# FFN batch norm of a decoder layer on one core: last statistics from PSUM, the average inside an expert product, and the fourth expert product behind the first scores

## The reference

```
xn   = layernorm(x)
q    = (xn @ Wq + bq) as (B, S, 8 heads, 64)
mean, var = moments of q over batch, token and head      # 64 features
q    = (q - mean) / sqrt(var + eps) * gamma + beta
s0, s1 = l2norm(q[:32]) . l2norm(key0), l2norm(q[32:]) . l2norm(key1)   # 32 + 32 scores per head
top 4 of each -> 16 pairs per head, softmax over the 16 sums -> weights w
eh   = gelu(down[idx] . xn)                 # exact gelu
out  = sum over heads and pairs of up[idx] * eh * w
x    = x + out
```

## Time and profile before

| | |
|---|---|
| median of 3 runs | 404.35 us (404.19 to 405.8) |
| span of the profiled execution | 403.8 us (a device time of its own is not given) |
| PE busy | 395.0 us (98%) |
| DVE, ACT, POOL busy | 300.1 us (74%), 237.8 us (59%), 215.9 us (53%) |
| the chain that ended last, by engine | PE 80%, POOL 12%, DVE 4%, issue 3%, DMA 1% |
| mean granted TensorE clock | 0.992 of full |

### The profile page before, as it was taken

How to read it: one execution, slowest core, us unless ns; L and a number is a source line. 1 busy time by engine, 2 the same in 40 slices (tenths; PEclk the granted TensorE clock), 3 DMA queues, 4 the chain that set the end, 5 groups by cost and what they waited for, 6 DMA issues and landing times.

```text
span 403.8 us, 7801 instructions
## 1 busy us (share of the span) xinstructions
PE 395.0 (98%) x2584; PEld 367.1 (91%) x2584; DVE 300.1 (74%) x1093; ACT 237.8 (59%) x519; POOL 215.9 (53%) x209
## 2 busy tenths in 40 slices
PE   8999999999999999999999999999999999999877
PEld 7878888899999999999999999999788899999766
DVE  5797768786757867476864848572986989899996
ACT  3886859454764466464545434342557977779462
POOL 1788999764385333153430300000166858989993
PEclk9999999999999999999999999999999969999999
DMA  7900213004434312233211000000100000000102
GB/s 226 310 2 1 83 55 102 8 11 128 128 89 121 118 30 59 58 84 104 65 47 30 2 0 2 1 2 2 27 1 2 0 2 2 28 28 27 41 28 67
DMA packets 19992, 21.38 MB, mean 53 GB/s; under 512 B 3180, under 2 KB 16624, under 8 KB 19952
## 3 DMA queue, kind: packets, MB, share of 16 engines
q1 hardware_dynamic: 18832, 19.96, 16.5%
q10 hardware_dynamic: 1120, 0.92, 0.7%
HBM read 18.78 MB, written 2.10 MB: 52 GB/s over the span
## 4 chain that ended last, share of the span: by engine, by line
PE 80%; POOL 12%; DVE 4%; issue 3%; DMA 1%; ACT 0%; SPq 0%; DVEq 0%; POOLq 0%; ACTq 0%
PE keep_pQ L75 11%; PE keep_pQ L76 11%; PE keep_pQ L77 11%; POOL ffn_prod L1258 9%; PE context_pA L1051 6%; PE context_pA L1053 6%; PE context_pA L1052 6%; PE context_pR L1085 6%; PE context_pR L533 3%; PE context_pA L533 3%; POOL ffn_near L1326 2%; PE ffn_pK L1807 2%; PE context_pR L75 2%; PE context_pR L77 2%; PE context_pR L76 2%
## 5 line engine op out<-in xcount | busy, mean ns | idle before, releaser
L899 DVE TENSOR_TENSOR att_pTl<-context_pR,att_pTh 128x512 fp32r<-128x512 f32 x64 | 36.9, 586 | 29.8 <-ACT att_pTh L811 29.5
L811 ACT ACTIVATE att_pTh<-context_pR 128x512 fp32r<-128x512 f32 x64 | 32.1, 514 | 40.1 <-PE context_pR L1085 40.1
L1258 POOL TENSOR_TENSOR ffn_prod<-ffn_first,ffn_near 128x1024 f32<-128x1024 f32 (+1 forms) x29 | 54.1, 1885 | 2.1 <-DVE ffn_first L1684 2.1
L851 ACT ACTIVATE att_prob<-keep_pQ,att_nmax 128x1206 f32<-128x1206 f32 x16 | 20.3, 1269 | 35.9 <-DVE att_nmax L935 35.8
L930 DVE TENSOR_REDUCE att_mx<-keep_pQ 128x1 f32<-128x402 f32 x64 | 34.5, 564 | 6.9 <-PE keep_pQ L77 6.6
L1837 PE MATMUL ffn_pT<-keep_ident,ffn_prod 128*128 128x128 f32 x240 | 30.5, 283 | 3.7 <-POOL ffn_prod L1258 3.7
L1837 PEld LDWEIGHTS ffn_pT<-keep_ident,ffn_prod 128*128 128x128 f32 x240 | 28.6, 148 | 5.8 <-DVE ffn_hT L1717 4.8
L786 POOL TENSOR_TENSOR keep_rstd<-att_ve,keep_mhalf 128x4 f32<-128x4 f32 x3 | 3.0, 1007 | 55.9 <-DVE att_ve L989 55.9
L1085 PE MATMUL context_pR<-keep_ident,att_prob 128*128 128x128 f32 (+1 forms) x208 | 31.8, 272 | 0.2 <-DVE att_pTl L899 0.2
L1051 PE MATMUL context_pA<-att_pTh,att_cNh 128*128 128x256 f32 (+1 forms) x104 | 31.0, 298 | 0.0
L1051 PE MATMUL context_pA<-att_pTh,context_cNh 128*128 128x256 f32 (+1 forms) x104 | 30.9, 297 | 0.0
(11 more groups left out here) (336 smaller groups left out, 1300.3 us busy)
## 6 DMA issues: line engine op xcount, KB each, us to landing
keep_raw<-in_ctxT SPq DMA_DIRECT2D x24, 256.0 KB, 2.7
keep_raw<-in_ctx SPq DMA_DIRECT2D x24, 256.0 KB, 3.0
out<-keep_x SPq DMA_DIRECT2D x16, 128.0 KB, 1.7
keep_x<-in_x SPq DMA_DIRECT2D x3, 512.0 KB, 9.9
gru_wout<-in_W_out SPq DMA_DIRECT2D x1, 512.0 KB, 8.7
keep_raw<-in_fWq SPq DMA_DIRECT2D x2, 256.0 KB
keep_raw<-in_ctxT SPq DMA_DIRECT2D x8, 32.5 KB, 3.1
keep_raw<-in_ctx SPq DMA_DIRECT2D x4, 65.0 KB
```

The source lines that it names most:

```text
L811: act.activation(to, bank, ACT.Copy).then_inc(bank_high, 1)
L899: dve.tensor_tensor(to, bank, half(it, 0, n)[0].bitcast(F32), ALU.subtract).then_inc(bank_free, 1)
L1258: return eng.tensor_tensor(prod[:, i % PB, a:b].rearrange("p h (i j) -> p h i j", j=KEYS), (factor if factor is not None else first[:, n % ...
```

## The change

The last query's statistics are taken from its PSUM bank before ACT evicts it; the bias, which the eviction adds, is added to the two means in the six numbers of the statistics. ACT's last eviction waits for that. The matmul of the average stands behind the second matmul of expert product 1. Expert product 3 stands behind scores 0 and 1; it is copied raw (`EARLY_GELU = 3`), and its Gelu is taken alone, behind the root of batch 3 in step 6 of ACT's loop. `squares(0)` stands between the second and the third chunk of group 1, and POOL squares each chunk of group 1 as it comes. Waits are renumbered to suit. `split_products` is written out in `expert_product`; its six matmuls and their order are the same.

```diff
@@ stage_ffn
+    last_stats = st.sem("last_stats")
-    EARLY_GELU = 4
+    EARLY_GELU = 3
@@ gpsimd
         for c in range(QC):
-            pool.wait_ge(q_ready_dve, QC + QC)
+            pool.wait_ge(q_ready_dve, QC + c + 1)
@@ scalar, evict(n)
+            if n == QS - 1:
+                act.wait_ge(last_stats, 1)
             act.activation(query(j, b * SEQ, (b + 1) * SEQ), pQ[:, n % 4], ACT.Identity,
@@ scalar
-        for m in range(EARLY_GELU - 1):
+        for m in range(DC):
             gelu(m)
...
         norm_roots(1)
+        expert_raw(EARLY_GELU)
         squared(2)
-        expert_raw(EARLY_GELU)
+        expert_raw(EARLY_GELU + 1)
         for i in range(TILES):
...
                     if n + 2 == BATCHES[k][-1]:
                         norm_roots(k)
+                        if k == 3:
+                            late_gelu(EARLY_GELU)
...
             if i == 1:
                 leftover(0)
-                for m in range(EARLY_GELU + 1, ES - 1):
+                for m in range(EARLY_GELU + 2, ES - 1):
                     expert_raw(m)
...
             if i == PER * BATCHES[-1][-1] - 2 * PER:
-                for m in range(EARLY_GELU, ES):
+                for m in range(EARLY_GELU + 1, ES):
                     late_gelu(m)
@@ vector, moments(n)
+            if n == QS - 1:
+                dve.wait_ge(query_mm, QS - QC)
+                dve.bn_stats(stats[:, n], pQ[:, n % 4]).then_inc(last_stats, 1)
+                dve.wait_ge(last_stats, 1)
+                means = stats[:, n, 1:6:3]
+                return dve.tensor_scalar(means, means, bq[:, n % QC:n % QC + 1], None, ALU.add)
@@ vector, normed()
             for c in range(QC):
+                if c == QC // 2:
+                    squares(0)
                 q = query(c, COLS, 2 * COLS)
...
@@ vector, weigh(i)
-            if i % (2 * TPB) == 0:
-                dve.wait_ge(gelu_ready, EARLY_GELU if i == 0 else ES)
+            if i % TPB == 0 and i <= 2 * TPB:
+                dve.wait_ge(gelu_ready, (EARLY_GELU, EARLY_GELU + 1, ES)[i // TPB])
...
         normed()
-        squares(0)
@@ tensor, expert_product(m)
-            else:
-                pe.wait_ge(gelu_ready, m - 3)
-            split_products(pe, expert_bank(m), [...]).then_inc(expert_mm, 1)
+            elif m < 4 + EARLY_GELU:
+                pe.wait_ge(gelu_ready, m - 3)
+            else:
+                pe.wait_ge(expert_read, m - 3 - EARLY_GELU)
+            out, cols = expert_bank(m), slice(c * P, (c + 1) * P)
+            xs = xTs[b]
+            pe.matmul(out, dnh[:, 0, cols], xs[0][:, 0], start=True, stop=False)
+            pe.matmul(out, dnh[:, 0, cols], xs[1][:, 0], start=False, stop=False)
+            if m == 1:
+                pe.wait_ge(pair_ready, 4)
+                pe.wait_ge(mv_ready, 1)
+                pe.matmul(pB[:, 0:2], pair[:], mv[:], start=True, stop=True).then_inc(avg_mm, 1)
+            pe.matmul(out, dnl[:, 0, cols], xs[0][:, 0], start=False, stop=False)
...
@@ tensor
         expert_product(0)
         expert_product(1)
-        pe.wait_ge(pair_ready, 4)
-        pe.wait_ge(mv_ready, 1)
-        pe.matmul(pB[:, 0:2], pair[:], mv[:], start=True, stop=True).then_inc(avg_mm, 1)
         expert_product(2)
-        expert_product(3)
...
         scores(0)
         scores(1)
+        expert_product(3)
         expert_product(4)
         norms(1)
         scores(2)
         scores(3)
-        for m in range(EARLY_GELU + 1, ES):
+        for m in range(EARLY_GELU + 2, ES):
             expert_product(m)
...
                 if i == SUM:
-                    pe.wait_ge(expert_read, DC)
+                    pe.wait_ge(expert_read, DC + 1)
                 sum_heads(i - SUM)
```

More of the change, by code:

```diff
@@ L1200, in stage_ffn @@
         st.sem(n) for n in ("query_mm", "query_read", "expert_mm", "expert_read", "gelu_ready"))
-    mv_ready, avg_mm, bn_ready = st.sem("mv_ready"), st.sem("avg_mm"), st.sem("bn_ready")
+    mv_ready, avg_mm, bn_ready, last_stats = (st.sem(n) for n in ("mv_ready", "avg_mm", "bn_ready", "last_stats"))
     sq_ready, sq_pool, norm_mm, n2_ready, nroot_ready, ninv_ready = (
@@ L1792, in expert_product @@
                 pe.wait_ge(query_read, QS - 4 + m - 2 + 1 - EVICTED)
-            else:
-                pe.wait_ge(gelu_ready, m - 3)
-            split_products(pe, expert_bank(m), [
-                ((dnh[:, k, c * P:(c + 1) * P], dnl[:, k, c * P:(c + 1) * P]), (xTs[b][0][:, k], xTs[b][1][:, k]))
-                for k in range(DC)]).then_inc(expert_mm, 1)
+            elif m < 4 + EARLY_GELU:
+                pe.wait_ge(gelu_ready, m - 3)
+            else:
+                pe.wait_ge(expert_read, m - 3 - EARLY_GELU)
[8 more added lines that the diff above has]
+            pe.matmul(out, dnl[:, 0, cols], xs[0][:, 0], start=False, stop=False)
+            pe.matmul(out, dnh[:, 1, cols], xs[0][:, 1], start=False, stop=False)
+            pe.matmul(out, dnh[:, 1, cols], xs[1][:, 1], start=False, stop=False)
+            pe.matmul(out, dnl[:, 1, cols], xs[0][:, 1], start=False, stop=True).then_inc(expert_mm, 1)
         def norms(n):
```

## The result

The changed kernel took 406.97 us in the median of 10 runs (405.52 to 407.98), the kernel before 404.42 (404.06 to 406.06). The ratio is 1.0049 with a 95% interval of 1.0034 to 1.0065, slower by 2.0 us; between the medians lie 2.6. Run again beside the experiments it came to 407.54 against 404.91, ratio 1.0066 (1.0039 to 1.0093). The profiled execution has a span of 405.1 and took 407.01 in all; the span before was 403.8.

What follows compares the result with a forecast made beforehand. PE's order was taken to bound the kernel to about 366, then DVE, then POOL. Span 403.8 + 0.35 (average and norms 0) + 0.35 (norms 6) = 404.5, on the runs' scale 405.0; range 403.1 to 406.7.

Steps and rivals of the forecast that it cites:

- What bounds the kernel: PE in its given order to the last group's norms (about 366), DVE to tile 11, POOL from 373.8 on.
- Part 1: Last query's statistics from PSUM before its eviction: aggregate done 0.49 us earlier, the eviction 0.75 later.
- Part 2: Average inside product 1: DVE reads it 0.78 us earlier; price a PE gap of about 0.15 (0 to 0.4).
- Part 3: Product 3 behind the first scores: gap of 0.3 to 0.4 at norms 0; with the average's gap, norms 1-3 0.35 later.
- stall of 0.15 in the norms: First norms took 1.83 us, second 1.68, in the kernel before; the difference was to go, taking 0.15 off the gaps.
- Part 4: Gelu 3 alone at tile 6 adds a table load: squared(6) 0.45 us later, PE held 0.35 at norms 6.
- The drain of 1.38: Added table load would hold PE 1.4 us longer at norms 6, sum 406.5; chance 0.03.
- Rival C: PE's clock falls before 322, around norms 0 and scores 0 and 1: 1.7 to 3.4 us lost, 406.7 to 408.4; chance 0.07.
- D: The clock fall at 326.5 goes away or shrinks: near 402.3 us; chance 0.04.

Runs made afterwards that it cites:

- parts 1 and 2 alone: Kernel before with only the last statistics from PSUM and the average inside product 1: 405.51 us against 404.91, ratio 1.0014.
- product 7 moved: Kernel before with expert product 7 moved behind norms 3 and its raw copy behind the root of batch 2: 405.49 us, ratio 1.0011.
- Without the fillers: Kernel before without its 13 idle-filling matmuls at steps 3 and 4 of PE's loop: 406.67 us, ratio 1.0039.
- parts 3 and 4 alone: Changed kernel with statistics, last eviction and average as in the kernel before: 409.28 us, ratio 1.0108.
- filled: Product 3 and Gelu 3 moved, statistics and average as before, plus four unused matmuls ahead of norms 0: 407.86 us against 404.70, ratio 1.0077.
- the filler's 12 runs: Changed kernel with one unused 512-column matmul in the gap ahead of norms 0: 406.78 us, ratio 1.0042.

## Why the prediction was right or wrong

*Direction, size, range.* Slower was right. That it would lie within the 0.5% that I called no change held by a hair (0.49%) and not the second time (0.66%), and that was luck: the runs lost nearly as much again by the clock as by the gaps, and the sum has nothing for it. 405.0 was 2.0 low and the forecast's own range of 404.4 to 405.7 missed; the outer range ended at 406.7 against a median of 406.97 (by the ratio, on the 404.35 of before, 406.3).

*What bounds the kernel.* The step that all rests on, that before 327 a gain of DVE or ACT is worth nothing and a gap of PE is lost, held: DVE's idle at norms 1 and 3 in the profile after, parts 1 and 2 alone, product 7 moved. That PE works through to 366 by its own load, and that each microsecond lost on it ahead of 366 is lost at the end, was too much. Without the fillers PE waits for squares and POOL, and a fall of 3.4 us costs nothing by norms 6 when it stands at 328 to 331. I had read PE without a wait from an execution with a long fall; one without a fall has a wait of 0.65 for POOL at 337.91. The gaps that the change opens move norms 3 and 6, and DVE and POOL behind them, so they count all the same.

*Part 1.* Right but for one duration: bn_stats from PSUM took 0.70 as from SBUF, but the sum onto two means took 0.37, not 0.16, so the aggregate came 0.31 earlier against the first product (1.33 behind it, before 1.64) in place of 0.49, and the coefficients 0.62 in place of 0.78. The eviction started 0.79 later for the 0.75 written.

*Part 2.* Mis-sized: the loss at the average was put at 0.15 and is 0.30 (0.45 less the 0.15 that it cost before). The aggregate was done 0.18 later than I had it, which is about that.

*Part 3.* PE ended product 2 0.38 ahead of norms 0, and it took 0.07 from product to norms before too: a gap of 0.31 for the 0.35 written. The stall of 0.15 in the norms did not go (1.77 before and 1.78 after, from their start to that of the scores): I read a difference between the ends of chain rows as a stall. Together 0.64 for 0.35 (0.30 and 0.31, and no 0.15 to take off), inside the bounds of 0 to 0.8. Product 3 behind the scores gave back all of the gain at norms 1, as said.

*Part 4.* 0.37 for 0.35, by the mechanism as worked out (exponential 8 and squares 6 are 0.43 late, against the first product and less the 0.64, for the 0.45 written). The drain of 1.38 that the Trainium skill ("ScalarE: Activation LUTs", "What ACT_TABLE_LOAD costs") adds did not show: the load of 348.87 starts 0.02 behind the root, the Gelu starts 0.01 behind its end and the exponential 0.01 behind that of 351.56. One wrong line: that tile 4's weighing needs Gelu 3 only beyond 360. It is at 356.7 in the profile before; the Gelu at step 6 is ready for it, at step 7 it is not.

*Rival C* is where the prediction failed in size. The sum has no term for the clock. I priced an early fall at 7 in 100, as all or nothing and in place of the forecast. What the runs show is a change in how often the clock falls, on top of the gaps, and it makes 0.9 to 1.3 of the 2.3. One profile of the changed kernel has a fall at the place named, but its span is that of the profile without it. That a gap brings it is likely for the long one (parts 3 and 4 alone, filled and not), not shown; for the short gap of the changed kernel the filler's 12 runs don't settle it, and which of the gaps, if any, brings the runs of 0.987 and less stays open. The profile before, with its one long fall, was itself not the usual execution: its span is 403.8, the median span of the runs is some 403.0, and 23 of 82 had no fall at all. D was thus no gain to be had by the change but something the kernel before had in a quarter of its runs and the changed kernel lost.

The Trainium skill ("TensorE: Matmul & The Clock Gate", Part 1) calls the gate's window free-running. The runs agree as far as they go: one kernel shows mean clocks from 0.983 to 0.996, and profiles of it with one fall or two.

## What to carry to other kernels

Where an engine waits at a join, ask what it waits for before making its input earlier: an early input with the same work still ahead of the join only moves the wait. When PE's order is kept dense by filler matmuls, a new gap of a few tenths costs its length, and half clock may come more often beside it (here it did, but that the gaps brought it isn't shown); put work in it, or leave the order alone. Take the granted clock of every run before comparing medians: compare equal clocks for the length of the path, and the mix of clocks for the rest, and don't take one profile's missing waits for those of every execution.

## What the runs showed of the hardware that I had not expected

Filler matmuls can shorten a kernel: taking 13 of them away added 2.0 us to the median (ratio 1.0024 to 1.0055), and four more in a gap of 1.14 us left the median 1.4 lower, if anything. 24 of the 37 runs of the kernel before with a mean clock of 0.995 or 0.996 (3.4 us at half clock in some 403) are as short as those with none. A wait of PE of 1.5 to 1.6 us at 377 left the clock up, one of 2.46 was followed by a fall. A tensor_scalar on two strided elements, with its addend read from memory, took 0.37 us, where one on a single element with a constant took 0.16.
